# Attention's weighted sums one unit later, and the mean's addition moved to the front of the last sum

## The reference, cut to what matters

```python
for x in batches:                       # x: 512 x 256
    # attention: 16 heads of 16, a shared rotary part of 32, causal
    scores = (q_h @ k_h.T + q_rope @ k_rope.T) / sqrt(48);  w = softmax(causal(scores))
    x1 = x + norm(concat(w @ v_h) @ W_o)
    # feed-forward: relu(h)^2 with ternary weights and a small low-rank part
    x2 = x1 + norm(bitlinear(relu(fc(norm(x1)))**2))
    # mixer: 32 slots, 8 phases, cos and sin waves of a value, a scan over the tokens with decay, read by a query
    x3 = x2 + norm(silu(gather(scan(cos/sin waves) * query)) @ W_out)
    # feed-forward with biases
    out = x3 + norm(relu(norm(x3) @ W1 + b1) @ W2 + b2)
```

## Time and profile before

| | us |
|---|---|
| median of 3 runs | 1418.54 (1416.97 to 1419.03) |
| profiled execution, its own time | 1416.25 |
| its span, first to last instruction | 1414.4 |
| PE busy | 1228.1 (87%) |
| DVE busy | 1090.1 (77%) |
| ACT busy | 1047.3 (74%) |
| POOL busy | 333.9 (24%) |
| mean granted TensorE clock | 0.933 |

### The profile page before, as it was taken

One profiled execution on the slowest core, in us unless ns is written; L12 is line 12 of the kernel. 1 busy time (PEld: TensorE's weight loads), 2 busy tenths in 40 slices (PEclk: granted clock), 3 DMA queues, 4 the chain that ended last, 5 costly groups with the idle time before them and its releaser, 6 DMA issues.

```text
span 1414.4 us, 22664 instructions
## 1 busy us (share of the span) xinstructions
PE 1228.1 (87%) x7820; PEld 777.4 (55%) x7820; DVE 1090.1 (77%) x2259; ACT 1047.3 (74%) x2101; POOL 333.9 (24%) x317
## 2 busy tenths in 40 slices
PE   5988987997899998999899998999999988977447
PEld 2564664464546655556556764665655655533224
DVE  3683258979878998889878998899888988586930
ACT  4674589687986889588978889597959897448522
POOL 3942202320122300430133101320133001300101
PEclk9798997899999999999999999999999999977759
DMA  8401414232215121521415131521242040022100
GB/s 264 84 22 26 102 31 129 74 83 56 83 37 138 42 83 55 121 52 24 137 44 129 23 100 45 135 47 50 94 94 64 24 137 23 23 77 67 38 0 15
DMA packets 72018, 101.49 MB, mean 72 GB/s; under 512 B 10640, under 2 KB 44064, under 8 KB 71904
## 3 DMA queue, kind: packets, MB, share of 16 engines
q1 hardware_dynamic: 71904, 100.03, 27.1%
HBM read 74.31 MB, written 25.69 MB: 71 GB/s over the span
## 4 chain that ended last, share of the span: by engine, by line
PE 55%; DVE 18%; ACT 14%; issue 7%; DMA 2%; SPq 2%; POOL 1%; POOLq 0%; DVEq 0%; ACTq 0%
PE ps L866 19%; PE ps L876 15%; DVE work L1488 6%; PE ps L949 5%; PE ps L931 5%; DVE work L1411 4%; PE ps L923 4%; PE ps L1017 3%; ACT work L1184 3%; ACT work L1177 2%; ACT xnd L1120 2%; DVE work L1497 1%; SPq L622 1%; PE ps L858 1%; DVE work L1479 1%
## 5 line engine op out<-in xcount | busy, mean ns | idle before, releaser
L1488 DVE TENSOR_TENSOR_SCAN work<-work 128x512 f32<-128x512 f32 x256 | 309.2, 1241 | 42.7 <-ACT work L1244 40.7
L1177 ACT ACTIVATE work<-work 128x384 f32<-128x384 f32 (+3 forms) x512 | 264.4, 558 | 69.7 <-DVE work L1411 68.9
L1411 DVE CUSTOM_DVE_ANT_0 work<-ps,work 128x384 f32<-128x384 f32 (+3 forms) x512 | 227.9, 486 | 92.1 <-PE ps L923 89.3
L747 POOL TENSOR_TENSOR later_norms<-later_norms,singles 128x2 f32<-128x2 f32 x112 | 103.3, 923 | 731.7 <-ACT xnd L1120 408.9
L931 PE MATMUL ps<-ident,work 128*128 128x128 f32 x1280 | 202.7, 284 | 16.8 <-ACT work L1184 9.0
L931 PEld LDWEIGHTS ps<-ident,work 128*128 128x128 f32 x1280 | 152.3, 145 | 87.2 <-issue 44.8
L1184 ACT COPY work<-ps 128x512 f32<-128x512 f32 x300 | 170.8, 573 | 5.6 <-PE ps L931 5.4
L1497 DVE TENSOR_TENSOR work<-work 128x1024 f32<-128x1024 f32 x128 | 158.7, 1240 | 5.3 <-DVE x L1333 0.2
L923 PE MATMUL ps<-work 96*128 96x384 bf16 (+3 forms) x512 | 123.6, 308 | 9.2 <-ACT work L1184 4.5
L866 PE MATMUL ps<-led_xTd,wf 128*128 128x512 f32 x256 | 120.2, 623 | 4.2 <-issue 4.2
L866 PE MATMUL ps<-led_xTd,wfc 128*128 128x512 f32 x256 | 118.4, 595 | 1.0 <-ACT led_xTd L1104 0.8
(11 more groups left out here) (174 smaller groups left out, 1932.0 us busy)
## 6 DMA issues: line engine op xcount, KB each, us to landing
work<-values SPq DMA_DIRECT2D x64, 256.0 KB, 3.2
work<-ratios SPq DMA_DIRECT2D x64, 256.0 KB, 4.2
scratch<-work SPq DMA_DIRECT2D x32, 384.0 KB, 4.8
work<-scratch SPq DMA_DIRECT2D x64, 192.0 KB, 3.8
work<-scratch SPq DMA_DIRECT2D x64, 128.0 KB, 4.0
x_in<-x SPq DMA_DIRECT2D x8, 512.0 KB, 6.5
work<-scratch SPq DMA_DIRECT2D x64, 64.0 KB, 4.1
values<-work SPq DMA_DIRECT2D x16, 256.0 KB, 3.0
```

The lines of the kernel that those rows point to most:

```text
L1177: i = s_.activation(part_of, part_of, ACT.Exp, scale=-1.0, bias=nmax[:, row:row + 1])
L1411: i = v_.tensor_tensor_reduce(sc[:, n % 4, at:at + nk], out_of(b, name)[:, at:at + nk], base_of(qt), -SCORE_SCALE, BIG, ALU.add, ALU.min, ...
L1488: v_.tensor_tensor_scan(ring[:, at, m, :], pwr[:, slot, :], ring[:, at, m, :], 0.0, ALU.mult, ALU.add).then_inc(*scanned.one)
```

## The change

It has three parts.

1. `LAG_PV` 4 becomes 5 and `LAG_OT` 15 becomes 16: PV and OT stand one unit later in attention's chain.
2. A new item `gmean` of ScalarE, behind `gxT` 1, adds the mean to `x3` (both halves, two tiles each). `gsum` is one VectorE operation per tile, x3 = xnd * rstd + x3, and leaves ScalarE's and GpSimd's lists.
3. All five merged lists are new.

```diff
-LAG_T, LAG_PV, LAG_OT = 3, 4, 15
+LAG_T, LAG_PV, LAG_OT = 3, 5, 16
-    for n in range(ALL + 6):
+    for n in range(ALL + 7):
...
-                       ("gxT", 0), ("gnorm", 1), ("gxT", 1)] + [("gc", g) for g in range(HC)]) + head_items(b + 2) +
+                       ("gxT", 0), ("gnorm", 1), ("gxT", 1), ("gmean", 0), ("gmean", 1)] + [("gc", g) for g in range(HC)]) + head_items(b + 2) +
...
-        words = 28832
+        words = 28864
...
-        o_scaled = signal("o_scaled", 2)
+        o_meant = signal("o_meant", 2)
...
-                if item == "gsum":
-                    need(pool, o_scaled, b, n + 1)
-                    g_.tensor_tensor(x3[:, half_of(n)], x3[:, half_of(n)], xnd[:, half_of(n)], ALU.add).then_inc(*g_sum.one)
...
-                if item == "gsum":
-                    need(act, o_rstd, b, n + 5)
+                if item == "gmean":
                     for t in tokens_of(n):
-                        i = s_.activation(xnd[:, t, :], xnd[:, t, :], ACT.Identity, scale=rstds[2][:, t:t + 1],
-                                          bias=means[:, b % 4, t:t + 1])
-                    i.then_inc(*o_scaled.one)
+                        i = s_.activation(x3[:, t, :], x3[:, t, :], ACT.Identity, bias=means[:, b % 4, t:t + 1])
+                    i.then_inc(*o_meant.one)
...
+                if item == "gsum":
+                    need(dve, o_meant, b, n + 1)
+                    need(dve, o_rstd, b, n + 5)
+                    for t in tokens_of(n):
+                        i = v_.scalar_tensor_tensor(x3[:, t, :], xnd[:, t, :], rstds[2][:, t:t + 1], x3[:, t, :],
+                                                    ALU.mult, ALU.add)
+                    i.then_inc(*g_sum.one)
```

More of the change, by code:

```diff
@@ L158 @@
     "pe": "xT ckv q qr k kr v base S T PV OT attnT out fxT fc fproj zxT z total query gather oout gxT gc gproj prep",
-    "act": "ystats fstats fystats zstats oystats gstats gystats centre norm xT q k v S T PV attnT fnorm fxT fc znorm zxT z weights query turn fold cos sin silu gnorm gxT gc gsum ternary prep",
+    "act": "ystats fstats fystats zstats oystats gstats gystats centre norm xT q k v S T PV attnT fnorm fxT fc znorm zxT z weights query turn fold cos sin silu gnorm gxT gc ternary prep gmean",
     "dve": "stats ckv q qr k kr base S T OT sum fsum z weights ratio total rates turn frac scan mix gate silu "
-           "osum gystats ternary prep tables means late",
-    "pool": "stats q k ystats fstats fc fystats zstats oystats gstats gystats gsum ternary tables late",
+           "osum gystats ternary prep tables means late gsum",
+    "pool": "stats q k ystats fstats fc fystats zstats oystats gstats gystats ternary tables late",
     "sp": "fetch pieces group z kv ratio rates pw inv gsum",
```

## The result

| | us | runs |
|---|---|---|
| before | 1417.36 (1415.44 to 1420.12) | 14 |
| after | 1414.18 (1410.84 to 1416.66) | 14 |

The ratio is 0.9974, 95% interval 0.9966 to 0.9982: by it 3.7 us faster (2.6 to 4.8), by the medians 3.2, where 12.1 were forecast. The time lies in the range, the direction is right, the size is a third.

A forecast was written before the change was run, and what follows sets the result against it. TensorE was taken to bound the middle, and latency between in-order engines the tail. Terms -7 - 3 + 2 + 1.5 - 4.2 - 1.4 = -12.1 us, from 1416.25 to 1404.15, plus 2.3: 1406.4 us; range 1394 to 1421.

The forecast's parts named there:

- parts 1 to 4: Everything up to the second bias addition near 1205 us: later PV, start, last sum, table loads; together 6.5 us earlier.
- part 5: Tail after about 1205 us: gate0 of batch 6 and scan0 sooner (-6.5, -7), gate0 of batch 7 later (+9.3); sum -4.2.
- the end: Very end of the kernel: VectorE's last sum replaces ScalarE and GpSimd steps before the store; -1.4 us.
- Part 1: PV and OT one unit later: most of PV's 11.0 us of waits for ScalarE's copy in the middle vanish; -7 us.
- rival 2: Middle and start give nothing: TensorE's wait turns into one for scores or exponentials; 1416.5 us, chance 0.20.
- Part 4: Table loads on ScalarE: six more changes around cos4 of batches 2, 3 and 4; +1.5 us, bounds 0 and 7.7.
- Part 2: Start: eight preparation products move from the middle of attention 0 to its end, filling TensorE's idle time; -3 us.
- Part 3: Last sum moved to VectorE: +2 us for work not hidden, bounds 0 and 14.1, and -1.4 at the very end.
- Rival 3: VectorE's queue becomes the bound in the middle, stopped at each gsum; +15.3 us there, 1425.2 us in all, chance 0.13.

## Why the prediction was wrong

By stretches, against the profiled execution before:

| stretch | forecast | measured | from |
|---|---|---|---|
| up to the second bias addition near 1205, parts 1 to 4 | -6.5 | +1.98 | timeline |
| of it, TensorE's gaps at the start, 35 to 420 | -3 | -2.3 | 46.8 for 49.1 |
| of it, TensorE's gaps in the middle, 420 to 1150 | -3.5 | +3.0 | 42.5 for 39.6 |
| the tail to the last mix, part 5 | -4.2 | -4.3 | timeline |
| the end | -1.4 | -0.9 | rest of the span |
| sum | -12.1 | -3.2 | spans, 1411.2 for 1414.4 |

The runs give -3.7 (-2.6 to -4.8). The tail and the end came nearly as forecast. What lies ahead of them is 8.5 us off; TensorE's gaps up to 1150 have most of it (0.6 more for 6.5 less).

**Part 1 failed.** "so most vanish", "I take 7 of it": it took the end of a named wait for the end of a gap. The wait of PV did vanish, but somebody else must wait for the same copy, since the bank is the scores' next; that is rival 2's mechanism, and its first half is what the waits after show. In the middle the kernel before had, beside the 11.0 of the earlier trace rows, these two and 0.3 for the scores:

```profile
PE ps L931 <- ACT work L1184: 3.6, 9, 0.4
...
PE ps L958 <- ACT work L1184: 2.3, 5, 0.5
```

so all of TensorE's waits for this copy were 11.0 + 3.6 + 2.3 + 0.3 = 17.2 us, and are 12.4 + 4.3 + 3.8 = 20.5 now: 3.3 more, where 7 less were forecast. With the lags alone changed PV's wait passed to the scores in the same way. How much the lag is worth in time, apart from the order that came with it, stays open; the runs with PV moved in a fixed order measure something else.

**Part 4** had the count of loads right, and its price is not a safe way to price. "Its chain share of 14% makes 1.1; I take +1.5". A share of the chain says how often an engine happens to be last, averaged over all of its work; the place decides. Beside the six loads of the change TensorE works on, so even less than 1.5 shows there; the same number of loads placed ahead of uncovered copies costs 9.5 us (7.4 to 11.7), and 36 cost 1.78 each, so the upper bound of the loads' own time was no bound either. The Trainium skill's rule ("ScalarE: Activation LUTs", Table sets: group one table's calls before changing) was weighed beside the edit and given 2.2 us; the planted loads agree with it, and the loads of the change show no cost on TensorE. The drain that the Trainium skill adds to a load ("ScalarE: Activation LUTs", What ACT_TABLE_LOAD costs) does not show here either: the sine starts 1.30 us after the load began (643.08 and 644.38) and the copy directly behind it.

**Part 2** came at once and did not last. TensorE's work up to 420 us, from 420 to 600 and from there to 1150, in the kernel after:

```profile
0.00:420.00 420.00, 358.21 (x2449) 224.48 (x2450) 285.24 (x726) 308.96 (x640) 131.23 (x129) 0.92 0.32 84
420.00:600.00 180.00, 164.46 (x1134) 104.04 (x1133) 155.72 (x346) 147.18 (x295) 29.32 (x32) 0.98 0.36 90
600.00:1150.00 550.00, 523.01 (x3511) 337.30 (x3509) 487.42 (x1015) 455.29 (x909) 111.34 (x107) 0.98 0.28 72
```

and in the kernel before:

```profile
0.00:420.00 420.00, 355.09 (x2422) 225.54 (x2422) 281.94 (x720) 307.59 (x634) 131.15 (x124) 0.91 0.32 83
420.00:600.00 180.00, 167.59 (x1073) 109.14 (x1072) 157.74 (x306) 140.73 (x278) 43.23 (x41) 0.98 0.35 87
600.00:1150.00 550.00, 522.83 (x3595) 333.69 (x3595) 483.40 (x1041) 457.17 (x925) 118.38 (x113) 0.99 0.29 74
```

3.1 us ahead at 420, level at 600, level at 1150. The 3.1 us are lost before the first of the extra loads (603.29): TensorE's waits for ScalarE's copy from 420 to 600 are 3.4 us in the kernel before and 8.0 in the kernel after. From 600 to 1150, where the loads lie, they are 13.8 and 12.7, and TensorE's work is the same to 0.2 us.

**Part 3** had the wrong sign: +0.6 with the end was forecast, and putting the old sum back costs 4.5 us. The end came (0.88 us on VectorE for two engines in turn). Its cost on VectorE, 14.1 us of work, did not show; taking the additions from GpSimd and the scaling from the place behind the statistics was a gain I had put at nothing. Part of it shows in the scores' waits for ScalarE's copy (12.4 us with the new sum, 18.6 with the old); which of the moved operations brings it the runs don't separate. That the direction came out is luck: with the old sum the kernel stands at 1.0006 (0.9994 to 1.0018), no gain at all, so the whole gain hangs on the one part that was forecast as a loss. Rival 3, which put 15.3 us on exactly this, is refuted in this order, though the same sum put by hand into the old order did cost 13.8: what it costs depends on the order around it.

**Part 5** held in its sum, partly by luck. It left out the contention with GpSimd from 1209 on, some 6 us, and it had VectorE wait 5.6 us for cos6, fsum0 and fsum1; in the kernel after these waits are 1.3 us, as VectorE came to them late. With the squares on ScalarE they are 3.1 + 1.2 + 0.5 = 4.8, and the time is the same. Its hidden assumption, that gate0 of batch 7 limits the end, was half true: gate0 10.5 us sooner gave nothing until the bias addition behind it was moved.

## What to carry to other kernels

When a wait disappears, ask who else needs the same event (here the same copy, for the bank): unless that one has cover too, the wait only changes its row. Count all waits for that event together, before and after. Don't price an added instruction by its engine's share of the chain; look at what the other engines have to do at its place. Beside a group of dense work a table load showed no gap on TensorE, and ahead of an uncovered copy it cost 1.6 to 1.8 us. The same holds for an experiment that plants such an instruction: it prices the place where it was planted, and before its number is carried to another kernel, that kernel's trace has to show the same gaps. And a stage without filler work, such as a tail, can be walked; in a dense middle the sum of single terms went wrong by 8 us.

## What the hardware showed beyond that

GpSimd's squares slow VectorE. Beside them a pair of fractions took 2.20 us for 1.42, a pair of scans 3.97 for 2.33, a mix 1.88 for 1.23, and a pair of conversions with one tensor input 2.44 for 0.88; some 6 us in 16. The squares suffered as well: three took 4.77 us, and in the kernel before, beside an idle VectorE, four took 4.03. With the squares on ScalarE all of it was gone. The Trainium skill ("GPSIMD Engine Reference", Key points) says that the two engines share their interfaces to SBUF; the runs agree and give the size. It names VectorE instructions with two SBUF inputs or in a 2-port mode; which of the two the slowed conversions were no run here shows. In the kernel before, VectorE happened to idle just there, so the earlier gate0 ran into it.
